# State-space layer: the decays of odd states move from PSUM to an SBUF buffer, and each decay waits for the scan two states back

## What is computed

```python
xp = x @ x_proj_w.T                       # x: [1 batch row, 512 tokens, 256 inner channels]
dt_raw, B, C = xp[..., :1], xp[..., 1:D_STATE + 1], xp[..., D_STATE + 1:]   # D_STATE = 16
dt = softplus(dt_raw @ dt_proj_w.T + dt_proj_b)
dA = exp(einsum('bld,dn->bldn', dt, A))   # the decay of channel d and state n at each token
dBx = (dt * x)[..., None] * B[:, :, None, :]
def step(h, inp):
    dA_t, dBx_t, C_t = inp
    h = dA_t * h + dBx_t                  # one scan over 512 tokens for each channel and state
    y = einsum('bdn,bn->bd', h, C_t)
```

## Time and profile before

| | |
|---|---|
| median of 3 runs | 2110.3 us (2090.95, 2110.3, 2113.36) |
| profiled execution, its own time | 2094.39 us |
| its span in the trace | 2092.3 us |
| state-space layer in it | about 530 to 1505 us of the span |
| busy over the whole span | PE 69%, DVE 67%, POOL 61%, ACT 45% |

### The profile page before, as it was taken

The page is one execution under the profiler, slowest core; times in us unless marked ns, Lnnn a source line. Parts: engine busy times, 40 slices in busy tenths (PEclk is TensorE's granted clock), DMA queues, the critical chain, the costliest instruction groups (busy, mean ns, idle before and its releaser), DMA issues.

```text
span 2092.3 us, 22136 instructions
## 1 busy us (share of the span) xinstructions
PE 1441.1 (69%) x5304; PEld 862.4 (41%) x5345; DVE 1403.7 (67%) x2613; ACT 948.0 (45%) x1612; POOL 1285.3 (61%) x927
## 2 busy tenths in 40 slices
PE   4777400443788888988888898887775629967671
PEld 3655300331343333433333343333454418867561
DVE  3666597111799989998998999899844403345454
ACT  2343100111655666655565665565433317755451
POOL 2111200672999889988999998898646650154644
PEclk8899655556899999999999999999987759989796
DMA  5333481231422333132233223242023116867572
GB/s 152 110 108 108 130 220 25 39 42 28 152 77 106 117 117 113 55 117 75 107 117 117 94 74 105 85 140 107 6 85 115 47 42 189 237 175 219 168 201 74
DMA packets 215243, 229.75 MB, mean 110 GB/s; under 512 B 24456, under 2 KB 182216, under 8 KB 210760
## 3 DMA queue, kind: packets, MB, share of 16 engines
q1 hardware_dynamic: 192392, 203.28, 30.5%
q0 software_dynamic: 22784, 25.71, 6.0%
HBM read 168.37 MB, written 62.95 MB: 111 GB/s over the span
## 4 chain that ended last, share of the span: by engine, by line
PE 34%; issue 20%; DVE 18%; another core or an unknown queue 9%; ACT 6%; POOL 4%; SPq 4%; DMA 3%; DVEq 1%; POOLq 0%; ACTq 0%
PE bank L1208 11%; DVE hst L1557 10%; PE bank L1163 5%; PE bank L1073 2%; DMA wv<-packed_weights 2%; PE bank L1161 1%; PE bank L1296 1%; PE bank L1313 1%; PE bank L1197 1%; SPq L583 1%; PE bank L1221 1%; PE bank L1299 1%; PE bank L1175 1%; PE bank L1322 1%
## 5 line engine op out<-in xcount | busy, mean ns | idle before, releaser
L1557 DVE TENSOR_TENSOR_SCAN hst<-bank,dbx 128x512 f32<-128x512 f32 x512 | 591.8, 1205 | 44.1 <-ACT bank L949 40.2
L752 POOL TENSOR_TENSOR dbx<-u,ball 128x1024 f32<-128x1024 f32 x256 | 617.8, 2497 | 4.8 <-POOL u L783 2.8
L1208 PE MATMUL bank<-prod,ident 128*128 128x512 f32 x1024 | 501.9, 625 | 32.6 <-DVE prod L1573 27.5
L949 ACT ACTIVATE bank<-dt,aneg 128x511 f32<-128x511 f32 x512 | 347.7, 688 | 309.6 <-DVE hst L1557 309.0
L1208 PEld LDWEIGHTS bank<-prod,ident 128*128 128x128 f32 x1024 | 201.9, 199 | 247.7 <-issue 196.5
L1573 DVE TENSOR_TENSOR prod<-hst,bank 128x1024 f32<-128x1024 f32 x192 | 233.5, 1216 | 18.2 <-DVE hst L1557 14.8
L814 POOL DMA_INDIRECT yg<-expert_rows,row_of x128 | 124.2, 970 | 167.4 <-DMA expert_rows<-yu 111.0
L761 POOL TENSOR_TENSOR prod<-hst,call 128x1024 f32<-128x1024 f32 x64 | 161.1, 2517 | 60.3 <-DVE hst L1557 60.2
L1597 DVE SCALAR_TENSOR_TENSOR hg<-bank,wv,ha 128x256 f32<-128x256 f32 x96 | 42.1, 479 | 154.1 <-ACT ha L1002 80.7
L1192 PE MATMUL bank<-parts,sel_c 128*128 128x512 bf16 x152 | 59.6, 394 | 105.5 <-DVE prod L1573 104.8
L647 POOL TENSOR_SCALAR rstd<-mv 128x4 f32<-128x4 f32 x16 | 3.7, 230 | 198.7 <-DVE mv L1377 198.7
(11 more groups left out here) (262 smaller groups left out, 2901.8 us busy)
## 6 DMA issues: line engine op xcount, KB each, us to landing
ball<-b_rows SPq DMA_DIRECT2D x32, 2048.0 KB, 7.1
wv<-packed_weights SPq DMA_DIRECT2D x96, 322.0 KB
call<-b_rows SPq DMA_DIRECT2D x16, 1024.0 KB, 9.5
xr<-sorted_rows SPq DMA_DIRECT2D x48, 256.0 KB
expert_rows<-yu SPq DMA_DIRECT2D x48, 256.0 KB
xg_rows<-xg SPq DMA_DIRECT2D x16, 320.0 KB, 2.6
xt<-in_x SPq DMA_DIRECT2D x16, 256.0 KB, 3.0
xT<-in_xT SPq DMA_DIRECT2D x16, 256.0 KB, 3.3
```

The source lines that it names most:

```text
L752: gp.tensor_tensor(dbx[n % NDB][:, :, :], u[s.par][:, :, :], ball[:, n:n + 1, :].to_broadcast([P, NH, SEQ]), ALU.mult).then_inc(dbx_rdy, 1)
L949: act.activation(da_ps[h][:, 1:SEQ], dt_[s.par][:, h, 1:SEQ], ACT.Exp, scale=aneg[:, h, n:n + 1]).then_inc(da_rdy, 1)
L1208: last = mm(y_ps[:, h, :], ident[:, :], from_[:, h, :], start=False, stop=(n == NS - 1), skip_group_check=True)
L1557: dve.tensor_tensor_scan(h_of[:, h, :], da_ps[h][:, :], dbx[n % NDB][:, h, :], 0.0, ALU.mult, ALU.add).then_inc(scan_rdy, 1)
```

## The change

A new SBUF tensor `da_odd` holds both halves of the decays of odd states. `da_of(n, h)` chooses it for odd n and the PSUM bank for even n, on ACT as output and on DVE as first input of the scan. As two consecutive states now have different buffers, ACT waits for the scan of state n-2 instead of n-1. Column 0 of the new buffer is set to zero once, in two more instructions.

```diff
+            da_odd = mb("da_odd", [P, NH, SEQ])
...
+        da_of = lambda n, h: da_odd[:, h, :] if n % 2 else da_ps[h][:, :]
...
                 for h in range(NH):
-                    need(act, scan_rdy, s.at(NS * NH, NH * (n - 1) + h + 1))
-                    act.activation(da_ps[h][:, 1:SEQ], dt_[s.par][:, h, 1:SEQ], ACT.Exp, scale=aneg[:, h, n:n + 1]
+                    need(act, scan_rdy, s.at(NS * NH, NH * (n - 2) + h + 1))
+                    act.activation(da_of(n, h)[:, 1:SEQ], dt_[s.par][:, h, 1:SEQ], ACT.Exp, scale=aneg[:, h, n:n + 1]
                                    ).then_inc(da_rdy, 1)
...
                         for h in range(NH):
                             dve.wait_ge(da_rdy, s.at(NS * NH, NH * n + h + 1))
-                            dve.tensor_tensor_scan(h_of[:, h, :], da_ps[h][:, :], dbx[n % NDB][:, h, :], 0.0, ALU.mult,
+                            dve.tensor_tensor_scan(h_of[:, h, :], da_of(n, h), dbx[n % NDB][:, h, :], 0.0, ALU.mult,
                                                    ALU.add).then_inc(scan_rdy, 1)
...
                 dve.memset(da_ps[h][:, 0:1], 0.0)
+                dve.memset(da_odd[:, h, 0:1], 0.0)
```

## The result

The changed kernel takes 2356.9 us (median of 4 runs, 2348.0 to 2363.4) against 2111.8 us for the kernel before (4 runs): a ratio of 1.119, with an interval of 1.114 to 1.124. It is 245 us slower; 2375 was forecast, in a range of 2130 to 2490. The profiled execution took 2348.0 us.

What follows compares the result with a forecast made beforehand. The period was taken as PE, then ACT, then DVE in the state-space layer. Whole-instruction exclusion added 237 or 322 us to 2094.4, giving 2331 and 2416; about 2375 was taken as the middle, range 2130 to 2490.

Steps and rivals of the forecast that it cites:

- What bounds the kernel: State-space layer: PE, then ACT, then DVE set the period, 60.9 us a sequence; POOL has 3.8 us of slack.
- Earlier decays: ACT may run one state ahead of the scans: near 5 us gained, since ACT is busy through the stretch.
- The rival in which the large wait goes away: DVE's wait for state 12's decay vanishes, no price for the input: 40.2 us gained, 2070 by the median; chance 0.04.
- Decays to SBUF: ACT's odd decays take 0.6 to 1.06 us each, taken as 0.69; at most 12 us in all.
- Scans with two SBUF inputs, by themselves: On DVE the place of the input alone gains or loses nothing; a line through two scans gives 2.03 ns per element.
- Scans beside POOL: Odd scans and POOL's SBUF-reading instructions exclude each other whole: 2347 to 2432 us, reaching 2490 with slower PE; chance 0.60.
- The rival of turns by the element: DVE's odd scans and POOL alternate element by element: 5.4 us a sequence, 2197 us by the median; chance 0.20.
- that of no price: Second SBUF input costs nothing beside POOL; only 5 us gained from earlier decays, 2105 us by the median; chance 0.16.
- The two sums: Whole-instruction exclusion in the layer counted by POOL's time and by DVE's: 2331 and 2416 us, by the median 2347 and 2432.
- The sum of DVE's time: POOL gets in between an odd pair's two scans: 81.0 us a sequence, 20.1 more, 322 us in all.
- POOL's time: If an odd pair's second scan keeps its turn: 50.8 + 18.6 + 6.3 = 75.7 us a sequence, 237 us more in all.
- PE's clock: With PE less busy its clock may fall: a tenth is 5 us a sequence, 80 in all, in the upper end.

Runs made afterwards that it cites:

- the last experiment: The changed kernel with one scan of 1024 elements for both halves of an odd state instead of two of 512: ratio 1.072 to the kernel before.
- the kernel with half a pair: The changed kernel with only the second half of odd states' decays in SBUF and the old wait for state n-1: ratio 1.058 to the kernel before.

## Why the prediction was right, point by point

**What bounds the kernel.** Right as far as it was tested: the POOL that only writes shows that POOL was no bound, and the move of Ln shows that ACT's stretch was one. PE's part was not tested. That the rest of the span is not touched holds as far as can be told, with the 16 us behind the last scan left unexplained.

**Earlier decays, 5 us.** Right, 5 us (0.3%) between the two kernels with a POOL that only writes. The rival in which the large wait goes away is out for this change; 31 us of it come with another edit, which shortens what ACT has to do ahead of that decay.

**Decays to SBUF.** 719 ns for an odd decay, 683 for an even one in the same trace; I took 690. Nothing waits for it.

**Scans with two SBUF inputs, by themselves.** Right: 1208 against 1205 ns beside a POOL that writes. The line through one scan of each kind could not have shown it, as it has no pair of one size.

**Scans beside POOL.** The mechanism is right: whole instructions exclude each other. Sorting the single scans of the last experiment by the time since the start of the large POOL instruction in progress (105 of 128 meet one; the other 23 take 2.26 to 2.28 us) gives the law directly: in the first 0.2 us after its start a scan takes 2.12 us more than 2.27 (mean of 12), at 0.8 to 1.0 us 1.37 (12), at 1.4 to 1.6 us 0.78 (24), at 2.0 to 2.2 us 0.08 (13). It waits for what is left of POOL's 2.31 us. The rule of the Trainium skill (SBUF — State Buffer, "Who interferes with whom"), an exclusive lock that the first to start holds for the whole instruction, is what these 105 meetings show, in both directions, and the kernel with 1208 ns agrees with its clause that a GpSimd instruction that only writes doesn't contend. Who comes next when an instruction waits is another matter, and there the order of starting did not always decide (see the last section). The rival of turns by the element is out, as is that of no price.

**The two sums.** The sum of DVE's time has the mechanism that the traces show, POOL getting in between two scans, and is too large: 81.0 us a sequence against 75.5. Its term for the first scan of a pair was 1.16 x 0.81 = 0.94 us; first scans wait 0.98 us in the mean in the changed kernel. The term for the second was 2.31 x 0.81 = 1.88 us, and this is the one that was mis-sized: they wait 1.31 in the mean, 80 of 128 a whole instruction (2.1 us) and 48 not at all. The trace tells them apart. In all 80, POOL's next large instruction had started before the first scan ended. In the 48 none had: in 31, at states 1 and 7, it was the product L763, which itself has to wait for this pair, and in 17, nearly all at state 15, a small instruction of the layer norm came first. So it was the order of POOL's program that decided, 5 pairs of 8, and not its share of the time. With the measured waits the sum is 58.4 + 8 x 2.29 = 76.7 us; the 1.2 us to 75.5 were not followed up.

POOL's time, 75.7 us, hits the measured 75.5 by luck. Its condition, that the second scan of a pair keeps its turn, fails in 80 of 128 pairs. It left out the waits and added POOL's other work of 6.3 us, which in fact runs beside scans or is overlapped by them: the kernel with one scan for both halves would need 50.8 + 18.2 + 6.3 = 75.3 us by that sum and takes 70.2. The floor is POOL's readings plus odd scans, 50.8 + 18.6 = 69.4 us in the changed kernel.

That the forecast came so near is luck in part as well. The 2375 is the middle of 2331 and 2416, the two sums for the profiled execution; by the median of the runs, 2347 and 2432, it is 2390, or 33 us over the 2357 measured. It is the mean of one sum that is too large and one that is right for a wrong reason, and the 16 us behind the layer, which no term foresaw, closed part of the gap.

**PE's clock.** The granted clock fell from 0.96 to 0.90 in the layer, and PE is busy 903 us there instead of 822 (530 to 1742 us). PE's share of the chain that ended last fell from 34 to 13% of the span, so it seems that little of it counts; it was not tested by itself.

## What to carry to other kernels

When DVE and POOL both run full, as here, the place of one operand decides whether they run side by side. Count the DVE instructions with two SBUF inputs beside a POOL instruction that reads; the reading times of both engines together are a floor. The waits of DVE grow with the number of turns: 18 us a sequence in 16 turns, 8 in 8 turns over the same elements. And before more buffers are given to a producer, look at what it is doing while its consumer waits: if it is busy all the way, a buffer buys nothing, but the order of its queue may.

## What was not expected of the hardware

- Turns are not fair. A waiting scan can be passed by three POOL instructions in a row (8.03 us), at state 9 in 12 of 16 sequences of the kernel with half a pair. The changed kernel has a milder case that makes up 39 of the 125 us for which its first scans wait: at state 7 in 14 of 16 sequences the first scan starts while POOL issues a DMA (L730), 0.01 to 0.19 us ahead of the next dbx, and yet lets the dbx go first and waits 2.7 to 2.9 us, longer than any reading instruction lasts by itself. What decides the order stays open; no kernel was run for it. One of the 14:

```profile
868.21 1.33 POOL L730 DMA_DIRECT2D rin<-resid_rows  x1
...
869.07 5.07 DVE L1559 TENSOR_TENSOR_SCAN hst<-da_odd,dbx 128x512 f32<-128x512 f32 x2
869.09 2.84 POOL L754 TENSOR_TENSOR dbx<-u,ball 128x1024 f32<-128x1024 f32 x1
```

- Even the smallest POOL instructions wait: `TENSOR_SCALAR` of 4 elements takes 0.57 us in the mean in the changed kernel's layer, 0.23 before, and 1.02 where it meets an odd pair. Each is a step of the layer norm, and its input, which DVE makes, comes later too: POOL waits 39.6 us for it ahead of the last sequence's, 3.9 before.
- An `Exp` of 511 elements takes 36 ns longer into SBUF than into PSUM (719 against 683 ns in one trace).
